# Softplus of two channel groups together in the first pass of a fused FFN, Mamba and FFN kernel

## The reference

```
x = x + 0.5 * ffn(layernorm(x))         # ternary weights, x is (4096, 1024)
x = x + mamba(layernorm(x))
x = x + 0.5 * ffn(layernorm(x))

mamba: u, z  = split(x @ W_in.T)
       u     = silu(conv4(u) + conv_b)
       dt_r, B, C = split(u @ W_xproj.T)            # 64, 16, 16
       dt    = softplus(dt_r @ W_dt.T + b_dt)       # (tokens, 1024)
       h_t   = exp(dt * A) * h_(t-1) + dt * B * u   # 16 states a channel
       y     = (sum(h * C) + u * Dskip) * silu(z)
       out   = y @ W_out.T
```

## Time and profile before

| what | value |
|---|---|
| time, median of 3 runs | 3271.41 us (3269.67 to 3273.12) |
| span of the profiled execution | 3268.6 us |
| first pass, from the start to the barrier | about 1109 us |
| one full iteration of the first pass | about 116 us |
| PE busy over the span | 2496.3 us (76%) |
| DVE busy | 2817.1 us (86%) |
| ACT busy | 1748.4 us (53%) |
| POOL busy | 1770.5 us (54%) |

### The profile page before, as it was taken

One profiled execution on the slowest core, in us unless ns is written; L12 is line 12 of the kernel. 1 busy time (PEld: TensorE's weight loads), 2 busy tenths in 40 slices (PEclk: granted clock), 3 DMA queues, 4 the chain that ended last, 5 costly groups with the idle time before them and its releaser, 6 DMA issues.

```text
span 3268.6 us, 41805 instructions
## 1 busy us (share of the span) xinstructions
PE 2496.3 (76%) x12320; PEld 1443.0 (44%) x12320; DVE 2817.1 (86%) x3588; ACT 1748.4 (53%) x3158; POOL 1770.5 (54%) x1499
## 2 busy tenths in 40 slices
PE   3577988988987366777787777777877777778777
PEld 1233434443433144454454454444544444445444
DVE  5565776776666599999999999999999999999994
ACT  2335675676657655555555555555554555554542
POOL 1111222222211367777777677777776777777773
PEclk8689999999988577988889889888898898898989
DMA  6543323332322522212121121121221221212101
GB/s 213 210 156 118 123 97 111 113 127 90 113 103 78 218 96 68 68 43 72 57 78 68 55 82 69 43 73 56 78 70 55 75 76 43 71 56 78 42 26 39
DMA packets 145153, 286.70 MB, mean 88 GB/s; under 512 B 32448, under 2 KB 81856, under 8 KB 140544
## 3 DMA queue, kind: packets, MB, share of 16 engines
q1 hardware_dynamic: 144896, 283.68, 25.1%
HBM read 174.06 MB, written 109.58 MB: 87 GB/s over the span
## 4 chain that ended last, share of the span: by engine, by line
POOL 25%; issue 23%; DVE 16%; PE 1%; POOLq 1%; DMA 0%; ACT 0%; DVEq 0%; SPq 0%
POOL dbu L1015 19%; DVE h L1185 9%; DVE y L1195 5%; POOL x L1041 2%; POOL o L1047 1%; POOL y L1037 1%; POOL carry L1028 1%; POOL dbu L1021 1%; PE p_g L1320 1%; POOLq L40 1%; DVE tokt L1217 1%; PE p_g L1310 0%; POOL small L69 0%; DVE q L1208 0%; DMA edge_dt<-dt_scratch 0%
## 5 line engine op out<-in xcount | busy, mean ns | idle before, releaser
L1104 ACT ACTIVATE p_da<-dt,neg_a 128x256 f32<-128x256 f32 (+1 forms) x2048 | 892.2, 468 | 934.1 <-DVE h L1185 933.1
L1185 DVE TENSOR_TENSOR_SCAN h<-p_da,carry,dbu 128x512 f32<-128x512 f32 x1024 | 1253.3, 1265 | 20.2 <-POOL dbu L1021 16.0
L1015 POOL TENSOR_TENSOR dbu<-dtu,bb 128x1024 f32<-128x1024 f32 x512 | 1197.2, 2360 | 1.7 <-issue 1.0
L1287 PE MATMUL p_ht<-ident,h 128*128 128x128 f32 x4096 | 658.9, 322 | 378.5 <-DVE h L1185 376.1
L1287 PEld LDWEIGHTS p_ht<-ident,h 128*128 128x128 f32 x4096 | 569.1, 167 | 494.9 <-issue 300.6
L1195 DVE SCALAR_TENSOR_TENSOR y<-p_ht,ct,y 128x1024 f32<-128x1024 f32 x512 | 645.1, 1260 | 0.0
L1320 PE MATMUL p_g<-wo,tokt 128*128 128x512 f16 x1536 | 357.2, 391 | 3.3 <-DVE tokt L1217 3.3
L706 PE MATMUL p_u<-xz,wu 128*128 128x512 f16 x1536 | 350.3, 386 | 0.0
L1329 PE MATMUL p_g<-wz,xz 128*128 128x512 f16 x1536 | 349.4, 385 | 0.0
L1028 POOL TENSOR_TENSOR carry<-h,carry_factor 128x8 f32<-128x8 f32 x254 | 52.3, 206 | 516.2 <-DVE h L1185 514.5
L358 POOL TENSOR_TENSOR late<-dt,u 128x512 f32<-128x512 f32 x64 | 82.4, 1287 | 425.4 <-DVE dt L550 425.4
(11 more groups left out here) (113 smaller groups left out, 2753.0 us busy)
## 6 DMA issues: line engine op xcount, KB each, us to landing
bb<-b_scratch SPq DMA_DIRECT2D x128, 256.0 KB, 3.2
xin<-in_x SPq DMA_DIRECT2D x32, 512.0 KB, 4.3
x_scratch<-x SPq DMA_DIRECT2D x32, 512.0 KB, 3.3
xz_scratch<-xz SPq DMA_DIRECT2D x16, 1024.0 KB, 5.8
y_scratch<-late SPq DMA_DIRECT2D x32, 512.0 KB, 2.9
dt_scratch<-dt SPq DMA_DIRECT2D x64, 256.0 KB, 2.2
dtu_scratch<-late SPq DMA_DIRECT2D x64, 256.0 KB, 2.5
dt<-dt_scratch SPq DMA_DIRECT2D x16, 1024.0 KB, 5.8
```

The costliest lines, as they stand in the source:

```text
L1015: nc.gpsimd.tensor_tensor(state[:, 4 * f:4 * f + 4, :], dtu[par][:, 4 * f:4 * f + 4, :], bb[n // NB % 2][:, n % NB:n % NB + 1, :].to_broad ...
L1104: ins_ = nc.scalar.activation(p_da[p % 2][:, k * T2 + k:(k + 1) * T2], dt[par][:, g, k:], ACT.Exp, scale=neg_a[:, g, n:n + 1])
L1185: nc.vector.tensor_tensor_scan(h[n % 2][:, 2 * p:2 * p + 2, :].rearrange("p g t -> p (g t)"), p_da[p % 2][:], dbu[n % 2][:, 2 * p:2 * p + ...
L1287: mm = nc.tensor.transpose(p_ht[t][:, g * P:(g + 1) * P], h[n % 2][:, g, t * P:(t + 1) * P], ident[:])
```

## The change

ACT does Relu, Abs and Exp of an even group and goes on; with the odd group, after its Exp, it does the two Ln of both. `s_units_before`, which DVE, POOL and SP use, gives nothing where the phase before ended with an even group, and both groups of the pair where it ended with an odd one. So the pair (0, 1) is worked off by DVE, POOL and SP in step 1 phase 3, (2, 3) in step 2 phase 1, (4, 5) in step 3 phase 1, (6, 7) in step 3 phase 3; before, groups 0 to 7 stood in phases 1.1, 1.3, 2.0, 2.1, 2.3, 3.1, 3.2, 3.3 (step.phase).

```
         def s_units_before(j, phase):

-            if phase:
-                return s_units(j, phase - 1, "d")
-            return s_units(j - 1, 3, "d") if j else []
+            seen = s_units(j, phase - 1, "d") if phase else s_units(j - 1, 3, "d") if j else []
+            return [(v, kind, e) for v, kind, g in seen if g % 2 for e in (g - 1, g)]
...
                             nc.scalar.activation(ex[g % 2], ex[g % 2], ACT.Exp, scale=-1.0).then_inc(exp_done, 1)
-                            wait(act, exp_done, q + 1)
-                            nc.scalar.activation(lg[g % 2], ex[g % 2], ACT.Ln, bias=1.0).then_inc(ln_done, 1)
+                            if g % 2:
+                                for e in range(2):
+                                    wait(act, exp_done, q + e)
+                                    nc.scalar.activation(lg[e], ex[e], ACT.Ln, bias=1.0).then_inc(ln_done, 1)
```

## The result

The changed kernel takes 3311.8 us (median of 4 runs, 3310.2 to 3318.7) against 3271.0: a ratio of 1.0128, 95% interval 1.0113 to 1.0142, 41 us slower. The forecast was 3277.5 in a range to 3291. The sign of the likeliest case was right, the size was not, and the time lies outside the range.

The account below looks back on a forecast made before the run. PE was taken to bound the first pass, through its holes. Iterations 2 to 5 +2.7, 1 +3.9, 6 +0.5, 7 +2.3, 8 -3.3 sum to +6.1 us: span 3274.7, median 3277.5, range 3265 to 3291.

Parts of the forecast that it names:

- the likeliest case: Whole kernel: slower, chance 0.49, against 0.39 for the same and 0.12 for faster.
- The bound and the holes: First pass: PE leads, busy 101.9 of 116.2 us an iteration; its 14.3 us of holes can be won or lengthened.
- the one on POOL: POOL's products, 1.29 us each, two in a row, are not awaited; costed at nothing, as were SP's stores.
- a gain of 0.85 in step 2: DVE in step 2 gains 0.85 us, as POOL's product starts later than L557 and 0.1 us of Ln waits go.
- the replay: One iteration replayed with old spacings, every engine in its order: y0 84.87 us after step 1's FFN product, before 84.25.
- The rival: Longer hole ahead of y0 lowers PE's clock, slowing step 0's FFN product 1.3 us an iteration: +9, 3286 us, chance 0.26.
- 7.1 (2.7 + 3.9 + 0.5): Full iterations' added time: 2.7 us for iterations 2 to 5, 3.9 for iteration 1, 0.5 for iteration 6.
- Relu's new wait: ACT's Relu waits for DVE's dt: group 2 for group 0's, 2.0 us; group 6 for group 4's, 3.4 us.
- The last pair: End of step 3: group 6's DVE work, 2.51 us, stands ahead of u*Dskip; y0 later, iteration 0.6 us longer.
- Iteration 8: Softplus alone at the first pass's end: 41.9 us becomes 38.6, a gain of 3.3, about 9 a pair.
- Removed loads: ACT's table loads: 32 fall away at Ln and 4 at Exp, 36 in all, 51 us of ACT; silu's 43 stay.
- the rival that silu needs no load behind an Exp: If Exp's set holds silu, eight more loads an iteration go, one ahead of `xt`: about 3266 us, chance 0.04.

Follow-up runs that it names:

- the run with the product held: Changed kernel, but POOL makes the even group's dtu product only once DVE has made dt of the odd group too: 3293.3 us, ratio 1.0072.
- the filled pair: Changed kernel and kernel before, each with unread matrix products in PE's three longest holes of each full iteration: 3304.0 us and 3264.5 us.
- held and filled: Changed kernel with POOL's even-group product held until dt of the odd group, and PE's three holes filled with 20, 12 and 8 unread products: 3283.4 us.
- the filled kernel before: Kernel before with 11, 16 and 12 unread matrix products in PE's holes, ahead of y0, step 2's FFN product and its turn 1: 3264.5 us.
- All three together: Changed kernel with POOL's product held, PE's holes filled (24, 12, 12) and four buffers for Relu's and Exp's results: 3270.0 us, ratio 0.9992.
- four buffers: Changed kernel with four buffers instead of two for Relu's and Exp's results, so Relu waits for dt of group g-4: 3292.1 us, ratio 1.0067.

## Why the prediction was wrong

**The bound and the holes** were read rightly: most of the loss and of the gains went through PE's waits, the rest through its low clock, and the loads saved were worth 19 us of the 51 that ACT was to be relieved of.

**The step that failed** is the one on POOL: "POOL has the same products (1.29 us each), two in a row, which aren't awaited [...] I cost both at nothing". They aren't awaited, but the first runs beside DVE's work of the odd group. The rows of before held the sign of it: I read L557's 1.20 us as a collision with POOL's product, took its going as most of a gain of 0.85 in step 2, and didn't ask which operation of DVE would stand beside the product after the move. The term measures +18.5 us by the run with the product held. In step 2 it shows as it is: from L500 of `xt` to x1 DVE takes 12.9 us before (669.56 to 682.48), where the replay had 12.1 for the changed kernel, and there it takes 13.3 (689.41 to 702.68), with one stretched operation in it. The Trainium skill, page "SBUF — State Buffer", section "Who interferes with whom", says that a DVE instruction with two inputs in SBUF contends with a GpSimd instruction that reads SBUF; L544 has two such inputs and stops, so by that rule the trace agrees. It would have given this rival beforehand.

**The clock.** This is the second term that was at nothing. The rival saw it, at the hole ahead of y0, and it came there: from y0 to step 1's FFN product the changed kernel takes 33.1 to 33.2 us in iterations 3 to 5, where the kernel before takes 31.9; filled, the two take 31.1 to 32.2. The replay also let go of the low stretch in step 3's FFN product, since DVE set the pace there, and put none into the other places where the changed kernel has holes, turn 1 of step 2 above all (1.97 us instead of 1.09). By the filled pair the clock costs the changed kernel about 5 us more than the one before in the full iterations; the rival had 9 in all.

**What is left.** Of the 34.3 us missing, 18.5 are the collision, 9.8 what the filling takes off beside it, and 5.9 stay. The 5.9 don't measure the rest of the replay, since filling also removes what the clock costs the kernel before. In the full iterations, held and filled against the filled kernel before, it is 697.1 to 681.6: the order of the work with Relu's waits costs 15.5 us, where the replay had 7.1 (2.7 + 3.9 + 0.5) against the unfilled one. All three together leave 4.6 of them, so most of the 15.5 goes with Relu's waits (the two runs differ a little in the filling too).

**Relu's new wait** was in the replay, 2.0 and 3.4 us an iteration; it is 2.24 ahead of group 2 and 3.44 ahead of group 6 in the trace, and four buffers give 19.6 us. Its length was priced rightly, but it was weighed as a footnote to the hole of 4.24: with four buffers the FFN product of step 2 comes 2.3 us earlier, so without the wait the relief of ACT would have arrived.

**The last pair** was named as the place where the deferred work is awaited (+2.5 us ahead of y0 an iteration). The place is right: it alone costs 24 us. The replay's 0.6 an iteration came out because gains of steps 1 and 2 were set against it, and these the collisions and the low clock ate; in the kernel with the product held and the holes filled, three of four iterations come within 0.6 us of the replay's distance.

**Iteration 8** gave 0.6 and not 3.3: the product stands beside all four odd groups there too, and the even groups' Relus wait 1.0 to 2.7 us for dt. In the profiles holding the product alone takes 0.9 us off this stretch and four buffers alone 2.8, so the wait weighs more. The pairs take 8.9, 9.1 and 10.7 us where the replay had about 9; the third has group 4's work behind a copy of y for which DVE waits 2.2 us for PE. **Removed loads** were right: 36 fewer. Silu's 43 stay, which rules out the rival that silu needs no load behind an Exp.

## What to carry to other kernels

When work is moved on one engine, ask what runs beside it afterwards on the other engines, on GpSimd where the work is VectorE's: an operation of 1.4 us that nobody awaits cost its neighbour 0.94 us each time. Table loads are saved as well by pairing units that already follow each other; that moves no other engine's work, and here it turned a loss of 1.3% into a gain of 0.9%. Defer work only out of phases whose end is not awaited: three pairs of four paid for themselves, and undoing the one ahead of the step that PE waits for took off 39 of the 41 us. And when idle time is filled to test a clock, compare only the stretches that have the hole: elsewhere the filling costs time.

## What the runs showed of the hardware that I had not expected

A VectorE tensor_tensor of 128x512 fp32 with both inputs in SBUF takes 0.69 us alone and 1.63 beside a GpSimd tensor_tensor of the same size that started ahead of it, and ends some 0.55 us after that one; with a second GpSimd product behind the first, the next VectorE operation takes 1.56 to 1.65 too. A VectorE tensor_scalar of this size (u*Dskip) takes 0.48 alone and up to 1.50 beside such a product. GpSimd's product takes 1.26 to 1.29 alone and 1.41 to 1.61 in the collisions with the odd groups, so the loss is mostly VectorE's. ScalarE's second Ln behind a first needs no load and starts 0.52 us after it: the pair takes 1.15 us.
